# GNN kernel, last node stage: the output stores move from ACT to SP, one gated half from ACT to DVE, and one POOL add is halved

## The chip, the cores and the metric

The kernel runs on one core of a Trainium2 chip. The metric is the device time of one execution in microseconds (us). A core has five engines that run their own instruction streams and wait for one another through semaphores: TensorE (PE), VectorE (DVE), ScalarE (ACT), GpSimd (POOL) and SyncE (SP), which here only issues transfers. 16 DMA engines move the data between HBM and the on-chip memory (SBUF). PE writes its results to PSUM, which DVE and ACT can read.

## What is computed

Four graph layers follow each other. Each adds a message-passing term to the 50,000 node rows of 160 floats, and normalizes the rows:

```python
x = _layernorm(x + _L0_gnn_ref(x, ...))
x = _layernorm(x + _L1_gnn_ref(x, ...))
x = _layernorm(x + _L2_gnn_ref(x, ...))
x = _layernorm(x + _L3_gnn_ref(x, node_vec1, node_vec1_n2, node_vec1_n3, ...))
return x
```

In the last layer the part that a node computes from its own row is gated by two scalars of the node, `node_attr` and `node_crystal_attr`:

```python
def fctp_scalar_attr(xs, xv, attr, Ws, Wv):
    s = xs * attr @ Ws
    v = jnp.einsum('nuc,uo->noc', xv * attr[:, :, None], Wv)
    return (s, v)
ssa, sva = fctp_scalar_attr(xs, xv, node_attr, Ws_sc_a, Wv_sc_a)
ssc, svc = fctp_scalar_attr(xs, xv, node_crystal_attr, Ws_sc_c, Wv_sc_c)
s_s, s_v = (ssa + ssc, sva + svc)
...
agg = jax.ops.segment_sum(edge_feat, edge_dst, num_segments=n) / np.sqrt(NUM_NEIGHBORS)
...
out_s = C_S * s_s + C_X * o_s
out_v = C_S * s_v + C_X * o_v
```

So a new row is: old row + summed messages + attr0 * (x W_a) + attr1 * (x W_c), and then the layer norm over its 160 columns.

## The kernel before

Each layer has an edge stage (98 pairs of edge tiles) and a node stage. The change touches only the node stage of the last layer (`l == 3`). It works on 100 blocks of 512 nodes; a block is a tile of 128 partitions with four rows of 160 columns side by side (`BT = 4`, index `j` or `t`; row slot `j` is one node per partition). Old rows and later results of a block live in place in `xn`, a ring of eight blocks (`NRING = 8`), and the summed messages in `an`, also a ring of eight. Both are views of the SBUF tensor `arena`, so the profile names them `arena`.

Each engine has its own function of the block step `b`, and the code orders the work of different blocks within one step by hand, with lags. The steady steps are a hardware loop (`steps`, eight block steps in one loop body, 88 of the 100 blocks); the steps before and after it are written out. In the last layer:

- SP, `node_loads(b)`: waits until the store of block b-8 has landed (`stored`), loads the rows of block b into `xn` (L455, the internal table `x_after`), waits for `x_added` of block b-6, and loads the messages of block b+2 (L476, `aggregates`).
- PE, `node_products(b)`: transposes block b (L853), then multiplies block b-1 by the two weight matrices (L892, 16 matmuls). The products land in four PSUM banks, `bank[4]` to `bank[7]`, one for each row slot j; columns 0 to 159 of a bank belong to gate 0 (g = 0), columns 160 to 319 to gate 1. There is one set of banks: banks 4 and 5 may be overwritten after DVE has read them (`y_stt`), banks 6 and 7 after ACT has (`second_gated`).
- ACT, `node_copies(b)`: issues the store of block b-5 (L1020), copies the transposed block b to `nT` (L1024), multiplies the four halves of slots 2 and 3 of block b-1 by their gates and writes them to `second` (L1037, 128x160 each, named `same_all` in the profile), takes the square root for block b-3 (L1043, `std`), and normalizes slots 0, 1 and 2 of block b-4 (L1049, three instructions, `normed`).
- DVE, `node_vectors(b)`: adds the gated halves of slots 0 and 1 of block b to `xn` (`products`, four SCALAR_TENSOR_TENSOR, L1364), then in `statistics` of block b-1: the first of four bn_stats (L1380), then `inverse()` of block b-2 (L1341, waits for `std_ready`), two bn_stats, `negated_mean()` of block b-2 (L1346, writes `shift` from `mv` and `rstd`), the fourth bn_stats; then four bn_aggr (L1391).
- POOL, `add_both(b)`: normalizes slot 3 of block b-4 (L676, `last_normed`), adds the messages to all of block b (L682, 640 columns, `x_added`), and adds the two gates' results for slots 2 and 3 of block b-1 from `second` (L688 and L691, 320 columns each, `second_added`).

The square root that `inverse()` waits for in DVE's step b is the one that ACT takes in its step b+1, behind the gated halves of block b:

```python
def inverse():
    if l and within(b, late, NBLK + late):      # late is 2 in the last layer
        dve.wait_ge(std_ready, b + ((l - 1) * NBLK + 1 - late))
        nc.vector.reciprocal(rstd[:, ki, :], std[:, ki, :]).then_inc(rstd_ready, 1)
```

Of the kernel before, what the change touches and what calls it, by code (L numbers as in the profile page):

```python
# [38 lines left out]
X_EARLY = 4  # L39
XGR = 4  # L40
# [137 lines left out]
def build(nc, nodes, front, back_rows, gate_rows, pairs, first4, eattr, main, small, self_rows, mark_rows, out):  # L178
# [3 lines left out]
    with ctx:  # L182
# [185 lines left out]
        def node_count(l, b):  # L368
            return b + (l * NBLK + 1)
# [20 lines left out]
        def _(sp):  # L390
# [23 lines left out]
            for l in range(4):  # L414
# [36 lines left out]
                arows = agg.rearrange("(b p t) c -> b p (t c)", p=P, t=BT)  # L451

# [26 lines left out]
                def node_loads(b, k, turn):  # L479
                    if isinstance(b, int) and b == 0:  # L480
                        for n in range(A_LEAD[l]):
                            aggregate_load(n, n)
                    if not isinstance(b, int) or b >= X_EARLY:
                        wait(sp, stored[k], node_slot(l, k, turn - 1) * 16)
                        alone(sp, passed["sp"])
                        row_load(b, k)
                    if within(b, 0, NBLK - A_LEAD[l]):
                        aggregate_load(b + A_LEAD[l], (k + A_LEAD[l]) % NRING)

                steps(sp, 0, NBLK, NODE_STEADY if l else LOADS_STEADY, node_loads, NRING)  # L490
# [5 lines left out]
        def _(gp):  # L496
# [35 lines left out]
            for l in range(4):  # L532
# [136 lines left out]
                def add_both(b, k, turn):  # L669
# [13 lines left out]
                    if within(b, 1, NBLK + 1):  # L683
                        gp.wait_ge(second_gated, b)
                        gp.wait_ge(x_added, b + NBLK)
                        alone(gp, passed["gp"])
                        x = xn[:, place(kk)].rearrange("p (t c) -> p t c", t=BT)[:, 2:4]
                        gp.tensor_tensor(x, x, second[:, kk % XGR, 0:2], ALU.add).then_inc(first_added, 1)  # L688
                        gp.wait_ge(first_added, b)
                        alone(gp, passed["gp"])  # L690
                        gp.tensor_tensor(x, x, second[:, kk % XGR, 2:4], ALU.add).then_inc(second_added, 1)  # L691
# [223 lines left out]
        def _(act):  # L915
# [14 lines left out]
            for l in range(4):  # L930
# [76 lines left out]
                to = out if l == 3 else xtab[l + 1]  # L1007
                orows = to.rearrange("(b p t) c -> b p (t c)", p=P, t=BT)

                def node_copies(b, k, turn):  # L1010
                    if within(b, STORE_LAG[l], NBLK + STORE_LAG[l]):
                        kk, tt = back(k, turn, STORE_LAG[l], NRING)
                        done = b - STORE_LAG[l]
                        if not isinstance(b, int):
                            done = act.snap(done)
                        act.wait_ge(normed, node_count(l, b - STORE_LAG[l]))
                        if l == 3:
                            act.wait_ge(last_normed, b - (STORE_LAG[3] - 1))
                        alone(act, passed["act"])
                        act.dma_start(orows[bass.ds(done, 1)].rearrange("o p c -> (o p) c"), xn[:, place(kk)]).then_inc(stored[kk], 16)  # L1020
# [8 lines left out]
                    if l == 3 and within(b, 1, NBLK + 1):  # L1029
# [5 lines left out]
                        for g in range(2):  # L1035
                            for j in (2, 3):
                                last = nc.scalar.activation(second[:, kk % XGR, 2 * g + j - 2, :], bank[4 + j][:, g * F:(g + 1) * F],  # L1037
                                                            ACT.Copy, scale=attr[:, kk, j, g:g + 1])
# [18 lines left out]
        def _(dve):  # L1057
# [137 lines left out]
            for l in range(4):  # L1195
# [102 lines left out]
                def node_vectors(b, k, turn):  # L1298
# [50 lines left out]
                    def products():  # L1349
# [7 lines left out]
                        if l == 3:  # L1357
                            dve.wait_ge(sc_ready, base + 1)
                            for g in range(2):
                                for j in range(2):  # L1360
                                    if g == 1:
                                        dve.wait_ge(half_done, b * 2 + (j + 1))
                                    row = xn[:, place(k), j * F:(j + 1) * F]
                                    stt(out=row, in0=bank[4 + j][:, g * F:(g + 1) * F], scalar=attr[:, k, j, g:g + 1], in1=row,  # L1364
                                        op0=ALU.mult, op1=ALU.add).then_inc(half_done if g == 0 else y_stt, 1)
                            return
# [117 lines left out]
```

## Time and profile before

| | before |
|---|---|
| median of 3 runs | 3911.85 us (3908.62 to 3913.18) |
| the profiled execution | 3914.43 us, span 3912.6 us |
| busy share of the span | PE 89%, DVE 69%, POOL 64%, ACT 56% |
| last node stage, about 3482 us to the end | some 430 us, 11% of the span |
| its steady loop, 3520 to 3880 us | PE 292.85, POOL 322.35, ACT 287.19, DVE 267.56 us busy in 360 us |

The profile lists for one execution every instruction with its engine, its line and its start. "SPq" and "ACTq" are transfers that the SP and ACT queues issue; "idle before" is the time in which an engine stood still just before an instruction, and the name behind the arrow is what ended it. DVE and ACT instructions overlap their predecessor by a little, so a sum of durations is more than the time they take in a row.

### The profile page before, as it was taken

The page shows a single profiled execution, that of the slowest core. Times are in us where ns is not written, and L with a number is a line of the kernel's source. Part 1 is how long each engine was busy: PE and PEld are TensorE (multiplying, and loading weights), DVE is VectorE, ACT ScalarE, POOL GpSimd, SP SyncE. Part 2 cuts the span into 40 slices and gives each one's busy share as a digit, 9 for nine tenths or more (in the row PEclk, how much of TensorE's full clock was granted, in tenths as well). Part 3 has the DMA queues.
Part 4 walks back from the last instruction along what each step waited for, and adds up shares of the span by engine and source line. Part 5 has one row for each costly group of instructions (what it writes and reads, how often), then busy time and mean ns, then how long its engine had stood idle before and what let it go on. Part 6 is the DMA issues. An engine that isn't in the chain of part 4 may idle for free.

```text
span 3912.6 us, 103757 instructions
## 1 busy us (share of the span) xinstructions
PE 3477.1 (89%) x26652; PEld 3218.3 (82%) x26652; DVE 2710.7 (69%) x10501; ACT 2205.7 (56%) x6014; POOL 2489.7 (64%) x2969
## 2 busy tenths in 40 slices
PE   2799998666599999999979999999989999988886
PEld 2799997565499999877779999877779999987775
DVE  3577775888766666588856666588866666657776
ACT  0244443666544444477745555577756666657777
POOL 1477776888667777566667777400046666658887
PEclk9899998888799999999989999999989999999999
DMA  8622223777522222499822222388832222237775
GB/s 353 248 63 62 61 53 101 255 253 258 180 58 59 57 56 50 118 303 299 287 76 63 61 59 55 93 293 298 297 97 55 53 52 50 45 99 243 239 246 199
DMA packets 424012, 572.02 MB, mean 146 GB/s; under 512 B 218794, under 2 KB 242344, under 8 KB 419590
## 3 DMA queue, kind: packets, MB, share of 16 engines
q1 hardware_dynamic: 280742, 289.28, 25.3%
q10 hardware_dynamic: 61488, 166.57, 10.9%
q0 software_dynamic: 81680, 114.98, 10.8%
q8 instruction: 43, 0.70, 0.1%
q14 instruction: 59, 0.48, 0.0%
HBM read 356.01 MB, written 233.79 MB: 151 GB/s over the span
## 4 chain that ended last, share of the span: by engine, by line
PE 59%; ACT 11%; issue 10%; DVE 7%; DMA 5%; POOL 4%; ACTq 2%; DVEq 1%; POOLq 0%; SPq 0%
PE bank L771 17%; PE bank L804 13%; ACT arena L1049 6%; PE bank L814 5%; PE bank L761 4%; PE bank L827 3%; PE bank L824 3%; PE bank L778 3%; PE bank L819 3%; PE bank L796 3%; ACT same_all L1037 2%; POOL mark_ring L638 2%; DVE stats L1380 2%; ACTq L1020 2%; DVE arena L1373 2%
## 5 line engine op out<-in xcount | busy, mean ns | idle before, releaser
L558 POOL DMA_INDIRECT aggregates<-arena,meta x784 | 790.7, 1008 | 459.7 <-issue 252.1
L771 PE MATMUL bank<-same_all,msg 128*98 (+1 forms) x6272 | 758.6, 275 | 0.0
L545 POOL DMA_INDIRECT xg<-x_after,meta x588 | 585.8, 996 | 252.1 <-issue 247.4
L771 PEld LDWEIGHTS bank<-same_all,msg 128*98 128x98 f32 x6272 | 715.8, 167 | 0.1
L1049 ACT ACTIVATE arena<-arena,shift,rstd 128x160 f32<-128x160 f32 x1500 | 658.4, 513 | 64.1 <-DVE shift L1315 61.5
L961 ACT ACTIVATE w<-bank 1x162 f32<-1x162 f32 (+1 forms) x784 | 257.8, 329 | 741.5 <-PE bank L804 737.6
L804 PE MATMUL bank<-w,arena 98*128 98x32 f32 (+1 forms) x4704 | 628.3, 270 | 0.0
L804 PEld LDWEIGHTS bank<-w,arena 98*128 98x128 f32 x4704 | 590.1, 193 | 0.0
L1380 DVE BATCH_NORM_STATS2 stats<-arena 128x6 f32<-128x160 f32 x1600 | 454.3, 313 | 42.9 <-DVE arena L1373 8.9
L1024 ACT ACTIVATE nT<-bank 128x640 f32<-128x640 f32 x400 | 281.8, 705 | 330.3 <-PE bank L883 179.6
L1268 DVE TENSOR_TENSOR arena<-bank,yv 128x192 f32<-128x192 f32 x294 | 105.1, 358 | 477.9 <-PE bank L824 294.2
L883 PEld LDWEIGHTS bank<-sc_cols,nT 128*128 128x128 f32 x2400 | 329.3, 204 | 86.4 <-issue 86.4
L892 PE MATMUL bank<-sc_cols,nT 128*128 128x128 f32 (+4 forms) x1600 | 277.7, 327 | 77.7 <-DVE arena L1364 72.5
L892 PEld LDWEIGHTS bank<-sc_cols,nT 128*128 128x128 f32 x1600 | 240.2, 192 | 119.2 <-issue 98.0
L883 PE MATMUL bank<-sc_cols,nT 128*128 128x128 f32 (+1 forms) x2400 | 336.2, 286 | 0.0
L853 PE MATMUL bank<-ident,arena 128*128 128x128 f32 x2000 | 299.7, 283 | 32.1 <-DMA arena<-nodes 21.9
L1226 DVE COPY arena<-bank 98x512 f32<-98x512 f32 x392 | 268.7, 685 | 77.0 <-PE bank L771 64.4
L1373 DVE SCALAR_TENSOR_TENSOR arena<-bank,attr,arena 128x160 f32<-128x160 f32 x800 | 261.5, 378 | 66.3 <-PE bank L883 35.9
L761 PE MATMUL bank<-ident,xg 128*128 128x128 f32 x1176 | 208.2, 287 | 102.4 <-DMA xg<-back_rows,meta 52.1
L949 ACT ACTIVATE arena<-bank 98x512 f32<-98x512 f32 x392 | 232.0, 592 | 77.9 <-PE bank L771 77.6
L853 PEld LDWEIGHTS bank<-ident,arena 128*128 128x128 f32 x2000 | 241.9, 153 | 39.6 <-issue 38.8
L954 ACT ACTIVATE arena<-bank 128x128 f32<-128x128 f32 (+1 forms) x392 | 129.7, 331 | 235.7 <-PE bank L778 233.4
(156 smaller groups left out, 7264.2 us busy)
## 6 DMA issues: line engine op xcount, KB each, us to landing
arena<-aggregates SPq DMA_DIRECT2D x400, 324.0 KB, 4.1
x_after<-arena ACTq DMA_DIRECT2D x300, 320.0 KB, 3.9
arena<-x_after SPq DMA_DIRECT2D x300, 320.0 KB, 3.6
aggregates<-arena ACTq DMA_DIRECT2D x25, 1296.0 KB, 14.7
arena<-nodes SPq DMA_DIRECT2D x100, 320.0 KB, 3.9
out<-arena ACTq DMA_DIRECT2D x100, 320.0 KB, 3.8
same_all<-sorted_dst SPq DMA_DIRECT2D x7, 1792.0 KB, 10.9
aggregates<-arena,meta POOLq DMA_INDIRECT x784, 2.3
```

Source lines behind the costliest of these rows:

```text
L545: gp.indirect_dma_start(xg[:, k % XGR, 4 + t * F:4 + (t + 1) * F], None, xtab[l], at).then_inc(gathered[k], 16)
L558: gp.indirect_dma_start(agg, at, tot[:, kk % TRING, t, 0:AW], None, bounds_check=NP - 1, oob_is_err=False).then_inc(spread[kk], 16)
L761: last = nc.tensor.transpose(bank[0][:, c * P:(c + 1) * P], xg[:, k % XGR, 4 + c * CH:4 + (c + 1) * CH], ident[:, :])
L771: last = nc.tensor.matmul(bank[5 + t][0:MR, c * P:(c + 1) * P], msg[:, k2, t, c, :], same_all[:, bass.ds(here[t], P)], start=True, stop=True)
L804: last = nc.tensor.matmul(to, aggT[:, t, (d + 1) * P:(d + 2) * P], of, start=True, stop=True)
L853: last = nc.tensor.transpose(to[:, c * P:(c + 1) * P], xn[:, place(k), c * CH:(c + 1) * CH], ident[:, :])
L883: last = mm(A[:, o:e], turned_x[c], sc[l][:, o:e], start=fresh, stop=fresh or c == 3)
L892: return mm(two(bank[4 + j][:, 0:2 * F], F)[:, :, lo:hi], turned_x[c], W[:, :, at:at + hi - lo], **flags)
L1024: nc.scalar.activation(nT[:, k % 2, :], two_banks[k % 2][:, 0:5 * P], ACT.Copy).then_inc(nturned_out, 1)
L1049: last = nc.scalar.activation(row, row, ACT.Identity, bias=shift[:, kk, t:t + 1], scale=rstd[:, kk, t:t + 1])
L1373: last = stt(out=row, in0=ob[:, o:o + F], scalar=gate, in1=row, op0=ALU.mult, op1=ALU.add)
L1380: last = nc.vector.bn_stats(stats[:, ks % 2, j, :], xn[:, place(ks), j * F:(j + 1) * F])
```

## The change

Three pieces of work move, all in the last layer only.

1. SP issues the stores of the output. In its step b it waits for `normed` and `last_normed` of block b-7 (`OUT_LAG = 7`) and issues that store, and only then goes on to the wait, the load of block b and the message load that it had before. ACT issues no store in this layer.
2. The half g = 0 of slot 2 is no longer gated by ACT. DVE adds it to `xn` in place with a fifth SCALAR_TENSOR_TENSOR, behind its four. ACT gates the other three halves, in the order (g, j) = (0, 3), (1, 3), (1, 2), and waits before the last of them for DVE's fifth (`half_done`, which now counts three for each block).
3. POOL's first add covers slot 3 alone (160 columns), its second slots 2 and 3 as before (320 columns).

```diff
--- before.py
+++ after.py
@@ -37,6 +37,7 @@
 QUAD = 4
 NRING = 8
 X_EARLY = 4
+OUT_LAG = 7
 XGR = 4
 AW = 2 + F
 AW3 = 2 * F
@@ -449,6 +450,7 @@
 
                 xrows = xtab[l].rearrange("(b p t) c -> b p (t c)", p=P, t=BT)
                 arows = agg.rearrange("(b p t) c -> b p (t c)", p=P, t=BT)
+                out_rows = out.rearrange("(b p t) c -> b p (t c)", p=P, t=BT)
 
                 def row_load(b, k):
                     at = b if isinstance(b, int) else sp.snap(b)
@@ -480,6 +482,21 @@
                     if isinstance(b, int) and b == 0:
                         for n in range(A_LEAD[l]):
                             aggregate_load(n, n)
+                    if l == 3 and within(b, OUT_LAG, NBLK + OUT_LAG):
+                        kk, tt = back(k, turn, OUT_LAG, NRING)
+                        done = b - OUT_LAG
+                        if not isinstance(b, int):
+                            done = sp.snap(done)
+                        scaled, fourth = node_count(l, b - OUT_LAG), b - (OUT_LAG - 1)
+                        if not isinstance(b, int):
+                            scaled, fourth = sp.snap(scaled), sp.snap(fourth)
+                        sp.wait_ge(normed, scaled)
+                        alone(sp, passed["sp"])
+                        sp.wait_ge(last_normed, fourth)
+                        alone(sp, passed["sp"])
+                        sp.dma_start(out_rows[bass.ds(done, 1)].rearrange("o p c -> (o p) c"), xn[:, place(kk)]).then_inc(stored[kk], 16)
+                    if not within(b, 0, NBLK):
+                        return
                     if not isinstance(b, int) or b >= X_EARLY:
                         wait(sp, stored[k], node_slot(l, k, turn - 1) * 16)
                         alone(sp, passed["sp"])
@@ -487,7 +504,7 @@
                     if within(b, 0, NBLK - A_LEAD[l]):
                         aggregate_load(b + A_LEAD[l], (k + A_LEAD[l]) % NRING)
 
-                steps(sp, 0, NBLK, NODE_STEADY if l else LOADS_STEADY, node_loads, NRING)
+                steps(sp, 0, NBLK + (OUT_LAG if l == 3 else 0), NODE_STEADY if l else LOADS_STEADY, node_loads, NRING)
             for k in range(NRING):
                 sp.wait_ge(stored[k], 16 * 4 * node_uses[k])
 
@@ -684,11 +701,11 @@
                         gp.wait_ge(second_gated, b)
                         gp.wait_ge(x_added, b + NBLK)
                         alone(gp, passed["gp"])
-                        x = xn[:, place(kk)].rearrange("p (t c) -> p t c", t=BT)[:, 2:4]
-                        gp.tensor_tensor(x, x, second[:, kk % XGR, 0:2], ALU.add).then_inc(first_added, 1)
+                        x = xn[:, place(kk)].rearrange("p (t c) -> p t c", t=BT)
+                        gp.tensor_tensor(x[:, 3], x[:, 3], second[:, kk % XGR, 1], ALU.add).then_inc(first_added, 1)
                         gp.wait_ge(first_added, b)
                         alone(gp, passed["gp"])
-                        gp.tensor_tensor(x, x, second[:, kk % XGR, 2:4], ALU.add).then_inc(second_added, 1)
+                        gp.tensor_tensor(x[:, 2:4], x[:, 2:4], second[:, kk % XGR, 2:4], ALU.add).then_inc(second_added, 1)
 
                 def node_moves(b, k, turn):
                     if l and k % 2 == 0 and within(b, 0, NBLK):
@@ -1004,18 +1021,15 @@
                     nc.scalar.activation(waves[:, four, 1, :], trig[:, four, 0], ACT.Sin, scale=-1.0,
                                          bias=half_pi[:, :]).then_inc(sin_ready, QUAD)
 
-                to = out if l == 3 else xtab[l + 1]
-                orows = to.rearrange("(b p t) c -> b p (t c)", p=P, t=BT)
+                orows = xtab[min(l + 1, 3)].rearrange("(b p t) c -> b p (t c)", p=P, t=BT)
 
                 def node_copies(b, k, turn):
-                    if within(b, STORE_LAG[l], NBLK + STORE_LAG[l]):
+                    if l < 3 and within(b, STORE_LAG[l], NBLK + STORE_LAG[l]):
                         kk, tt = back(k, turn, STORE_LAG[l], NRING)
                         done = b - STORE_LAG[l]
                         if not isinstance(b, int):
                             done = act.snap(done)
                         act.wait_ge(normed, node_count(l, b - STORE_LAG[l]))
-                        if l == 3:
-                            act.wait_ge(last_normed, b - (STORE_LAG[3] - 1))
                         alone(act, passed["act"])
                         act.dma_start(orows[bass.ds(done, 1)].rearrange("o p c -> (o p) c"), xn[:, place(kk)]).then_inc(stored[kk], 16)
                     if within(b, 0, NBLK):
@@ -1032,10 +1046,11 @@
                         act.wait_ge(attr_copied, node_count(l, b - 1))
                         act.wait_ge(sc_ready, 2 * (b + l * NBLK))
                         alone(act, passed["act"])
-                        for g in range(2):
-                            for j in (2, 3):
-                                last = nc.scalar.activation(second[:, kk % XGR, 2 * g + j - 2, :], bank[4 + j][:, g * F:(g + 1) * F],
-                                                            ACT.Copy, scale=attr[:, kk, j, g:g + 1])
+                        for g, j in ((0, 3), (1, 3), (1, 2)):
+                            if j == 2:
+                                act.wait_ge(half_done, b * 3)
+                            last = nc.scalar.activation(second[:, kk % XGR, 2 * g + j - 2, :], bank[4 + j][:, g * F:(g + 1) * F],
+                                                        ACT.Copy, scale=attr[:, kk, j, g:g + 1])
                         last.then_inc(second_gated, 1)
                     if l and within(b, SQRT_LAG[l], NBLK + SQRT_LAG[l]):
                         kk, tt = back(k, turn, SQRT_LAG[l], NRING)
@@ -1359,10 +1374,14 @@
                             for g in range(2):
                                 for j in range(2):
                                     if g == 1:
-                                        dve.wait_ge(half_done, b * 2 + (j + 1))
+                                        dve.wait_ge(half_done, b * 3 + (j + 1))
                                     row = xn[:, place(k), j * F:(j + 1) * F]
                                     stt(out=row, in0=bank[4 + j][:, g * F:(g + 1) * F], scalar=attr[:, k, j, g:g + 1], in1=row,
                                         op0=ALU.mult, op1=ALU.add).then_inc(half_done if g == 0 else y_stt, 1)
+                            dve.wait_ge(sc_ready, base + 2)
+                            row = xn[:, place(k), 2 * F:3 * F]
+                            stt(out=row, in0=bank[6][:, 0:F], scalar=attr[:, k, 2, 0:1], in1=row,
+                                op0=ALU.mult, op1=ALU.add).then_inc(half_done, 1)
                             return
                         for d, tiles in enumerate(((3,), (0, 1, 2)) if l == 0 else ((0, 1), (2, 3))):
                             dve.wait_ge(sc_ready, base + (d + 1))
```

How the instructions stand on DVE in one step of the steady loop. Before, from the start of `products` to the first reciprocal (`arena<-bank,attr,arena` are the gated halves that are added to `xn`):

```order
L1364 SCALAR_TENSOR_TENSOR arena<-bank,attr,arena 128x160 [waits sc_ready]
L1364 SCALAR_TENSOR_TENSOR arena<-bank,attr,arena 128x160
L1362 REGISTER_ALU
L1364 SCALAR_TENSOR_TENSOR arena<-bank,attr,arena 128x160 [waits half_done]
L1362 REGISTER_ALU
L1364 SCALAR_TENSOR_TENSOR arena<-bank,attr,arena 128x160 [waits half_done]
L1401 REGISTER_ALU [waits second_added]
L1380 BN_STATS stats<-arena 128x6 [waits y_stt]
L1340 REGISTER_ALU
L1341 RECIPROCAL rstd<-std 128x4 [waits std_ready]
```

Now, from DVE's fourth to the same reciprocal:

```order
L1379 SCALAR_TENSOR_TENSOR arena<-bank,attr,arena 128x160 [waits half_done]
L1381 REGISTER_ALU
L1383 SCALAR_TENSOR_TENSOR arena<-bank,attr,arena 128x160 [waits sc_ready]
L1420 REGISTER_ALU [waits second_added]
L1399 BN_STATS stats<-arena 128x6 [waits y_stt]
L1355 REGISTER_ALU
L1356 RECIPROCAL rstd<-std 128x4 [waits std_ready]
```

The fifth (L1383) stands between the four and the reciprocal; nothing behind it has changed.

ACT in one step of the steady loop before, from the end of `normed` to the normalization (`same_all<-bank,attr` are the gated halves):

```order
L1018 REGISTER_ALU [waits normed]
L1020 ISA [waits last_normed]
L1020 DMA out<-arena 128x640
L1022 REGISTER_ALU
L1024 ACTIVATE nT<-bank 128x640 [waits sc_ready,nturned]
L1033 REGISTER_ALU [waits attr_copied,second_added]
L1037 ACTIVATE same_all<-bank,attr 128x160 [waits sc_ready]
L1037 ACTIVATE same_all<-bank,attr 128x160 x3
L1043 ACTIVATE std<-mv,eps 128x4 [waits mv_ready]
```

And now:

```order
L1036 REGISTER_ALU
L1038 ACTIVATE nT<-bank 128x640 [waits sc_ready,nturned]
L171 REGISTER_ALU
L1047 REGISTER_ALU [waits attr_copied,second_added]
L1052 ACTIVATE same_all<-bank,attr 128x160 [waits sc_ready]
L1052 ACTIVATE same_all<-bank,attr 128x160
L1051 ISA
L1052 ACTIVATE same_all<-bank,attr 128x160 [waits half_done]
L1058 ACTIVATE std<-mv,eps 128x4 [waits mv_ready]
```

The wait for `normed` and the store are gone, one gated half is gone, and the third waits for `half_done` with the square root behind it.

SP in one step of the steady loop before:

```order
L455 ISA [waits stored1]
L455 DMA arena<-x_after 128x640
L170 REGISTER_ALU
L476 ISA [waits x_added]
L476 DMA arena<-aggregates 128x648
```

And now:

```order
L495 REGISTER_ALU [waits normed]
L497 ISA [waits last_normed]
L497 DMA out<-arena 128x640
L457 ISA [waits stored1]
L457 DMA arena<-x_after 128x640
L171 REGISTER_ALU
L478 ISA [waits x_added]
L478 DMA arena<-aggregates 128x648
```

The store of block b-7 stands ahead of both loads, with its two waits, and all three go through SP's queue.

## Rows read from the trace of the kernel before

**Rows 1.** Busy time of each engine in a stretch, clock, DMA share: the steady loop.

```profile
3520.00:3880.00 360.00, 292.85 (x1860) 254.72 (x1859) 267.56 (x1237) 287.19 (x796) 322.35 (x399) 1.00 0.74 241
```

**Rows 2.** The output's stores in the loop: count, first and last start.

```profile
L1020 ACTq DMA_DIRECT2D out<-arena x88: 343/343/379, 3521.7 to 3876.3; - x88
```

**Rows 3.** Order of time, one block: start, length (us), engine, instructions, idle before.

```profile
3705.46 1.26 DVE L1364 SCALAR_TENSOR_TENSOR arena<-bank,attr,arena 128x160 f32<-128x160 f32 x4
...
3705.59 0.47 POOL L676 TENSOR_SCALAR arena<-arena,rstd,shift 128x160 f32<-128x160 f32 x1
3705.67 0.70 ACT L1024 ACTIVATE nT<-bank 128x640 f32<-128x640 f32 x1 [0.82 <-PE bank L892]
3706.03 1.43 POOL L682 TENSOR_TENSOR arena<-arena 128x640 f32<-128x640 f32 x1
3706.27 1.24 ACT L1037 ACTIVATE same_all<-bank,attr 128x160 f32<-128x160 f32 x4
...
3706.87 2.75 PE L892 MATMUL bank<-sc_cols,nT 128*128 128x256 f32 x16 [0.66 <-DVE arena L1364]
3706.88 0.33 SPq L455 DMA_DIRECT2D arena<-x_after  x1
3707.38 0.32 ACT L1043 ACTIVATE std<-mv,eps 128x4 f32<-128x4 f32 x1
...
3707.57 1.35 ACT L1049 ACTIVATE arena<-arena,shift,rstd 128x160 f32<-128x160 f32 x3
3707.74 0.18 DVE L1341 RECIPROCAL rstd<-std 128x4 f32<-128x4 f32 x1 [0.78 <-ACT std L1043]
3707.77 0.87 POOL L688 TENSOR_TENSOR arena<-arena,same_all 128x320 f32<-128x320 f32 x1 [0.31 <-ACT same_all L1037]
...
3708.27 0.39 DVE L1346 SCALAR_TENSOR_TENSOR shift<-mv,rstd 128x4 f32<-128x4 f32 x1
...
3708.82 0.86 POOL L691 TENSOR_TENSOR arena<-arena,same_all 128x320 f32<-128x320 f32 x1 [0.18 <-POOL arena L688]
3709.04 0.38 DVE L1391 BATCH_NORM_AGGREGATE mv<-stats 128x2 f32<-128x6 f32 x4
...
3709.22 0.35 ACTq L1020 DMA_DIRECT2D out<-arena  x1
3709.54 0.38 DVE L1364 SCALAR_TENSOR_TENSOR arena<-bank,attr,arena 128x160 f32<-128x160 f32 x1
...
3709.75 0.70 ACT L1024 ACTIVATE nT<-bank 128x640 f32<-128x640 f32 x1 [0.83 <-PE bank L892]
```

**Rows 4.** Who waited for whom in the steady loop: us in total, times, longest.

```profile
DVE rstd L1341 <- ACT std L1043: 66.5, 89, 1.1
PE bank L892 <- DVE arena L1364: 65.9, 88, 1.2
```

**Rows 5.** In order of time, the drain: from DVE's aggregates to ACT's root.

```profile
3901.30 0.38 DVE L1391 BATCH_NORM_AGGREGATE mv<-stats 128x2 f32<-128x6 f32 x4
...
3901.71 0.30 ACT L1043 ACTIVATE std<-mv,eps 128x4 f32<-128x4 f32 x1 [0.53 <-DVE mv L1391]
```

**Rows 6.** L1346, ns min/median/max: layers 1 and 2, then the steady loop.

```profile
L1346 DVE SCALAR_TENSOR_TENSOR shift<-mv,rstd x200: 141/145/174, 1640.8 to 2859.6; 128x4 f32<-128x4 f32 x100
...
L1346 DVE SCALAR_TENSOR_TENSOR shift<-mv,rstd x89: 331/387/394, 3520.7 to 3879.4; 128x4 f32<-128x4 f32 x89
```

**Rows 7.** A store, and the transposes behind the load that waited for it.

```profile
3701.09 0.34 ACTq L1020 DMA_DIRECT2D out<-arena  x1
...
3709.98 0.30 PE L853 MATMUL bank<-ident,arena 128*128 128x128 f32 x1 [0.36 <-DMA arena<-x_after]
```

**Rows 8.** Transfers issued in the loop: queue, count, KB each, median us to landing.

```profile
arena<-aggregates SPq DMA_DIRECT2D x88, 324.0 KB, 3.9
arena<-x_after SPq DMA_DIRECT2D x88, 320.0 KB, 3.1
out<-arena ACTq DMA_DIRECT2D x88, 320.0 KB, 3.9
```

## The prediction

> **What bounds the kernel now.** The change touches only the last node stage, so the busy shares of the whole span say little. I first read the busy times of its steady loop [rows 1] and the stores in it [rows 2]: 88 stores start from 3521.7 to 3876.3 us, so a block takes (3876.3 - 3521.7) / 87 = 4.076 us, and 360 us hold 88.3 blocks. Per block PE is busy 3.32 us, DVE 3.03, ACT 3.25, POOL 3.65. None fills 4.076, so the order within a block has to be read [rows 3].
>
> ACT first. Its rows follow each other without a gap that another engine makes: from the copy to nT (3705.67) to the gated halves 0.60, to the root (3707.38) 1.11, to the normalization (3707.57) 0.19, its three instructions 1.35 (to 3708.92), then 0.83 until the next copy at 3709.75. The sum is 4.08, the whole period. In the last 0.83 the queue waits for ACT's own `normed` and issues the store (3709.22). The row names PE, whose products end at 3706.87 + 2.75 = 3709.62; but by the code the copy of block b waits for the products of block b-2, which were through a period earlier. What stands directly ahead of the copy is the store. ACT's instruction stream sets the pace.
>
> The others wait for it. DVE's reciprocal waits for ACT's root in each block, 66.5 / 89 = 0.75 us; PE waits 0.75 us for DVE's adds [rows 4]; POOL's first add waits a little for the gated halves (0.31 idle in its row, of which some 0.17 is its own queue) [rows 3].
>
> One more thing matters. L1346 (`shift`) takes 0.145 us in layers 1 and 2, and 0.387 in this loop [rows 6]. In the order of time it runs from 3708.27 to 3708.66, and POOL's L688 ends at 3707.77 + 0.87 = 3708.64 [rows 3]. So DVE's instruction, which reads `mv` and `rstd` from SBUF, stands until POOL's add is through: 0.24 us on DVE's path in each block.
>
> The Trainium skill, "SBUF — State Buffer", section "Who interferes with whom", says that a DVE instruction with two SBUF inputs and a GpSimd instruction that reads SBUF exclude each other for a whole instruction, and that the one issued first wins. The rows here agree: 0.387 against 0.145.
>
> **The change part by part.** I count from the start of DVE's adds of a block (3705.46 in the rows) as 0.
>
> *ACT.* It loses the store with its wait (0.83 becomes about 0.1, by the distances between its other instructions) and one gated half ((1.24 - 0.40) / 3 = 0.28 us apart). Its own work is then 0.60 + 0.83 + 0.19 + 1.35 + 0.1 = 3.07 us per block. By itself this would free the whole loop.
>
> *DVE and the new wait.* The fifth add stands behind four that begin (1.26 - 0.38) / 3 = 0.295 us apart, so it begins at 1.18 and ends at 1.56. It waits for all of PE's products, which are done by then: they start 0.15 after DVE's fourth add of the block before and take 2.75 [rows 3], that is 1.41 + 2.75 = 4.16 after that block's 0, or 0.1 to 0.4 in this one. ACT's last gated half now waits for that fifth add. Behind it in ACT's stream stands the root, and for that root DVE's reciprocal waits *in the same step*. So there is a closed path:
>
> - fifth add ends: 1.56
> - ACT begins its last half: +0.03. The nearest row of a wait of ACT for DVE: the bn_aggr end at 3901.30 + 0.38 = 3901.68, the root starts at 3901.71 [rows 5]. Bounds: 0.03, and 0.15 as between DVE's fourth add and PE's products (3706.72 to 3706.87). I take 0.03, the same pair of engines.
> - the root starts 0.28 behind it and takes 0.32, the reciprocal starts 0.04 later (3707.70 to 3707.74): 2.23
> - from the reciprocal to the next block's adds: 1.80 today (3707.74 to 3709.54).
>
> With 1.80 the period would be 4.03, almost the 4.076 of today: the store's 0.83 is given back to the new wait.
>
> *POOL and `shift`.* But the 1.80 contain the 0.24 of waiting for L688. The add is now 160 columns wide. No row has that add; 640 columns take 1.43 and 320 take 0.87, which extrapolates to 0.59, and the 160-column normalization L676 takes 0.47 [rows 3]. I take 0.52, with these as bounds. ACT's last half starts at 1.59 and lasts 0.40; POOL starts 0.26 behind its end (3707.51 to 3707.77), at 2.25, and ends at 2.77 (2.72 to 2.84). `shift` is ready 0.53 after the reciprocal (3707.74 to 3708.27), at 2.76. So it meets the very end of that add or none, and waits 0 to 0.1 us. The second add starts 0.18 behind the first, at 2.95, when `shift` (0.145) is over. The 1.80 become 1.56, and the period 2.23 + 1.56 = **3.79 us**.
>
> *Is anything else slower than 3.79?* POOL: 3.65 busy less 0.35 for the halved add, plus two waits of 0.18 for its own results: 3.66. PE 3.32, DVE 3.03 + 0.3 = 3.33 plus small own waits, ACT 3.07. No, but POOL is near.
>
> *SP.* This is the cover that I cost at nothing. The store of block n now leaves when `normed` comes, as before: ACT ends its normalization at 1.59 + 0.28 + 0.19 + 1.35 = 3.41, and 0.3 for the wait (3708.92 to 3709.22) gives 3.71. Behind the store, and behind its waits, are queued the load of block n+7 and the messages, and PE waits for that load. An issue takes 0.33; with the waits I estimate 0.7 from store to load. The load lands 3.1 us after its issue, or 3.9 if it queues behind the store as the messages queue behind the load today [rows 8]: 7.5 to 8.3. PE must begin the transposes of block n+7 some 0.7 before the products of block n+6, which start 1.41 after the 0 of block n+5, two periods on: 7.58 + 1.41 - 0.7 = 8.3. It fits, with 0 to 0.8 us left. Every load also waits for the store eight blocks back: median 3.9 us to landing [rows 8], but one took 5.8 (3701.09 to the load at 3706.88), and PE then waited 0.36 at 3709.98 [rows 3, 7].
>
> The Trainium skill, "DMA: Bandwidth & Descriptors", section "Issuing engines are not separate DMA queues", holds that transfers share the same 16 engines whoever issues them, and that several issuers save only the issue time. By it the landing would not change with the queue (3.1, not 3.9); the sum is the same.
>
> *The sum.* 88 blocks x (4.076 - 3.79) = 25 us. The 12 blocks outside the loop have the same path; few of them run at full pace, and I give them 1 us. The profiled execution took 3914.4 (span 3912.6), so it would take 3888; the median of the runs is 2.6 lower, which gives **3886 us**.
>
> **The rivals.**
>
> *A, the forecast:* 3.79. Its own range: POOL's 3.66 on one side (-11 us); on the other the 0.15 for the wait (+0.12 x 88 = +10.6): 3875 to 3897. Chance 0.60.
>
> *B, the load is late but not much.* If each store landed after 5.8 us and the load after 3.1, as in the pair above, the transposes come 8.9 after the store of eight blocks back, and that must fit in three periods + 0.7 - 3.7: period 3.97, 3902 us. For it: such pairs occur. Against: they occur when SP issues two pairs of loads at once, and SP now goes in step with ACT; in the whole loop DMA has 0.26 of its time free [rows 1]. Chance 0.13.
>
> *C, no gain.* Either `shift` goes on waiting 0.24 us (POOL's add starts later than I think, because POOL comes late from its 640-column add), which gives 4.03 and 3908 us, or the waits on both sides cost 0.1 more each. Chance 0.15.
>
> *D, slower.* `shift` comes to POOL just after the second add has begun, and stands for all its 0.86. The point: POOL's first add and the 0.18 behind it must end before 2.76, so the first would have to take under 2.76 - 2.25 - 0.18 = 0.33 us; the nearest rows say 0.47 to 0.59. Price: a second add from 2.74 to 3.60, so `shift` ends at 3.62 instead of 2.90, the period is 3.79 + 0.72 = 4.51, and the time 3912 + 0.43 x 88 = 3950 us. Or the load queues (3.9) behind stores that take 5.8: 9.7, period 4.23, 3925 us. Chance 0.12 together.
>
> The skill's rule of exclusion, named above, is what makes D possible: by it the order of issue decides, and the wait is for a whole instruction.
>
> **How the numbers follow.** A measurement of this kernel can tell about 0.2% (8 us) from no change; that is 0.09 us per block, so a period under 3.99 counts as faster. A and B: faster 0.73; C: same 0.15; D: slower 0.12. The time is that of A. The range leaves out D and 0.05 below: 3877 to 3911.
>
> **What would show it.** In the loop after: stores 3.79 us apart; ACT idle before the last of three gated halves, waiting for DVE's fifth add, and no longer before nT; the reciprocal still waiting for the root, some 0.45 us (2.23 less the end of the bn_stats ahead of it, at 1.18 + 0.295 + 0.3); L1346 at 0.15 to 0.25 us instead of 0.387; PE's wait for DVE down to about 0.45. Wrong would be: L1346 at 0.39 or more, or PE or POOL waiting for loads in most blocks, or the 128x160 add far from 0.52.

## The result

| | before | after |
|---|---|---|
| median of the runs, us | 3911.85 (3908.41 to 3913.76, 5 runs) | 3886.79 (3882.35 to 3888.55, 5 runs) |
| span of the profiled execution, us | 3912.6 | 3886.7 |
| granted TensorE clock of the execution | 0.967 | 0.966 |

The ratio is 0.9936, 95% interval 0.9921 to 0.995: 25 us faster, where 26 were predicted. In another set of runs it was 0.993 (0.9916 to 0.9943).

First, the first section of the page of the changed kernel (busy time, share of the span, instructions), and its busy times in a stretch of the steady loop, in the columns of [rows 1]:

```profile
PE 3480.6 (90%) x26652; PEld 3220.3 (83%) x26652; DVE 2718.1 (70%) x10601; ACT 2187.9 (56%) x5914; POOL 2459.0 (63%) x2969
```

```profile
3520.00:3840.00 320.00, 277.61 (x1769) 242.06 (x1768) 258.69 (x1261) 258.21 (x672) 278.76 (x378) 1.00 0.76 260
```

In 100 us PE is now busy 86.8 us instead of 81.3, and POOL 87.1 instead of 89.5: the block got shorter, and POOL's share fell although it does more blocks. How long a block is can be read from any instruction that occurs once in it. For `shift`, in that stretch (minimum, median and maximum in ns, then the first and the last start):

```profile
L1361 DVE SCALAR_TENSOR_TENSOR shift<-mv,rstd x84: 143/145/148, 3523.4 to 3839.9; 128x4 f32<-128x4 f32 x84
```

That makes (3839.9 - 3523.4) / 83 = 3.813 us a block, against 4.076. Every block time below is this division, from the same kind of row. 88 x (4.076 - 3.813) = 23 us, nearly all of the gain. And `shift` takes 0.145 us instead of 0.387 [rows 6]: it never waits for POOL.

One block of the changed kernel in order of time, against [rows 3]:

```profile
3699.94 1.26 DVE L1379 SCALAR_TENSOR_TENSOR arena<-bank,attr,arena 128x160 f32<-128x160 f32 x4
...
3701.12 0.38 DVE L1383 SCALAR_TENSOR_TENSOR arena<-bank,attr,arena 128x160 f32<-128x160 f32 x1
...
3701.53 0.40 ACT L1052 ACTIVATE same_all<-bank,attr 128x160 f32<-128x160 f32 x1 [0.39 <-DVE arena L1383]
3701.82 0.29 ACT L1058 ACTIVATE std<-mv,eps 128x4 f32<-128x4 f32 x1
...
3702.14 0.18 DVE L1356 RECIPROCAL rstd<-std 128x4 f32<-128x4 f32 x1 [0.41 <-ACT std L1058]
3702.18 0.53 POOL L705 TENSOR_TENSOR arena<-arena,same_all 128x160 f32<-128x160 f32 x1 [0.33 <-ACT same_all L1052]
...
3702.67 0.15 DVE L1361 SCALAR_TENSOR_TENSOR shift<-mv,rstd 128x4 f32<-128x4 f32 x1
...
3702.88 0.86 POOL L708 TENSOR_TENSOR arena<-arena,same_all 128x320 f32<-128x320 f32 x1 [0.18 <-POOL arena L705]
3703.20 0.38 DVE L1410 BATCH_NORM_AGGREGATE mv<-stats 128x2 f32<-128x6 f32 x4
...
3703.70 1.26 DVE L1379 SCALAR_TENSOR_TENSOR arena<-bank,attr,arena 128x160 f32<-128x160 f32 x4
3703.72 0.36 SPq L497 DMA_DIRECT2D out<-arena  x1
...
3704.34 0.33 SPq L457 DMA_DIRECT2D arena<-x_after  x1
```

From 3699.94 to 3703.70 are 3.76 us. The closed path of the prediction stands in these rows: fifth add, ACT's last half 0.03 behind its end (3701.50 to 3701.53), root, reciprocal at 2.20, and 1.56 to the next adds. `shift` starts at 3702.67, 0.04 before the 160-column add ends (3702.71), and is over at 3702.82, 0.06 ahead of the start of the second add; it fits in between, narrowly. The chain that ended last (start, us, what) runs through the same places:

```profile
3704.88 0.38 DVE arena L1383
3705.58 0.29 ACT std L1058
3705.90 0.18 DVE rstd L1356
3706.08 0.44 DVE stats L1399 x2
```

The waits in the stretch, in the columns of [rows 4], and those of SP:

```profile
PE bank L909 <- DVE arena L1379: 39.1, 78, 0.8
ACT same_all L1052 <- DVE arena L1383: 35.4, 81, 0.8
DVE rstd L1356 <- ACT std L1058: 35.2, 84, 0.6
...
DVE arena L1379 <- issue: 4.9, 10, 0.5
...
PE bank L870 <- DMA arena<-x_after: 3.1, 4, 1.4
```

```profile
SPq L176 <- ACT arena L1064: 140.3, 84, 2.1
```

ACT now waits 35.4 / 81 = 0.44 us a block for the fifth add; the reciprocal waits 0.42 for the root instead of 0.75; PE waits 0.50 for DVE instead of 0.75, and only 4 times for a load. What the prediction does not have is the row "issue": 10 times in 84 blocks DVE's adds start up to 0.5 us late with no releaser. Two of those places are 3555.61 and 3586.05, eight blocks apart:

```profile
3555.61 1.26 DVE L1379 SCALAR_TENSOR_TENSOR arena<-bank,attr,arena 128x160 f32<-128x160 f32 x4 [0.50 <-issue]
3586.05 1.26 DVE L1379 SCALAR_TENSOR_TENSOR arena<-bank,attr,arena 128x160 f32<-128x160 f32 x4 [0.49 <-issue]
```

This is where the hardware loop of eight block steps turns. That block takes 4.13 us, the seven others 3.76, and the mean is 3.81. The kernel before has the same idle time (11 times, up to 0.5 us; there the profile names PE behind it), but its DVE waited 0.75 us for the root in each block anyway.

### The profile page after: what moved, and what is told of

The parts are those of the page before. It is cut to its first block, busy times and chain, and to the rows that moved or that the text cites. A ratio compares the mean times of both kernels' runs of the same rounds, so it can differ in the third digit from the quotient of the medians.

```text
span 3886.7 us, 104123 instructions
## 1 busy us (share of the span) xinstructions
PE 3480.6 (90%) x26652; PEld 3220.3 (83%) x26652; DVE 2718.1 (70%) x10601; ACT 2187.9 (56%) x5914; POOL 2459.0 (63%) x2969
## 4 chain that ended last, share of the span: by engine, by line
PE 59%; DVE 11%; issue 10%; ACT 7%; DMA 5%; POOL 4%; ACTq 1%; DVEq 1%; SPq 1%; POOLq 0%
PE bank L788 17%; PE bank L821 13%; PE bank L831 5%; ACT arena L1064 4%; PE bank L778 4%; PE bank L844 3%; PE bank L841 3%; PE bank L795 3%; PE bank L836 3%; DVE stats L1399 3%; PE bank L813 3%; POOL mark_ring L655 2%; DVE mv L1410 1%; ACT nT L1038 1%; DVE arena L1392 1%
```

## The experiments

The first four kernels ran on one chip beside the kernel before (3910.57 us there).

### One part alone

The first of two leaves only the stores on SP. Against the changed kernel, shortened (the fifth add itself goes too, and `half_done` counts two a block again):

```diff
-for g, j in ((0, 3), (1, 3), (1, 2)):
-    if j == 2:
-        act.wait_ge(half_done, b * 3)
+for g in range(2):
+    for j in (2, 3):
...
-dve.wait_ge(sc_ready, base + 2)
-stt(out=row, in0=bank[6][:, 0:F], ...)
...
-gp.tensor_tensor(x[:, 3], x[:, 3], second[:, kk % XGR, 1], ALU.add)
+gp.tensor_tensor(x[:, 2:4], x[:, 2:4], second[:, kk % XGR, 0:2], ALU.add)
```

> The change with only its first part: SP issues the output's stores; ACT gates all four halves and waits for nothing of DVE; POOL adds 320 columns twice. Theory (closed path through the fifth add and ACT's root, and POOL's narrower add frees shift): ACT's own work falls to 0.60 + 1.11 + 0.19 + 1.35 + 0.1 = 3.35 us per block, but POOL still needs 3.65 busy and two waits of 0.18, 4.01 us. So POOL becomes the bound, a period of 4.0 to 4.03, 3905 to 3908 us, nearly nothing gained; shift still waits (L1346's line at 0.3 or more). Rival 1 (the store on ACT was the whole price, so its removal is the whole gain): a period of 3.8, about 3886 us.

3887.89 us (3885.57 to 3889.47), ratio 0.9944 (0.993 to 0.9958). My theory was wrong, its rival right. POOL's rows in order of time show why:

```profile
3697.75 0.86 POOL L708 TENSOR_TENSOR arena<-arena,same_all 128x320 f32<-128x320 f32 x1 [0.18 <-POOL arena L705]
3698.56 0.21 POOL L591 COPY attr<-gate_all 128x24 f32 x1
3698.74 0.48 POOL L693 TENSOR_SCALAR arena<-arena,rstd,shift 128x160 f32<-128x160 f32 x1
3699.18 1.43 POOL L699 TENSOR_TENSOR arena<-arena 128x640 f32<-128x640 f32 x1
3700.57 0.86 POOL L705 TENSOR_TENSOR arena<-arena,same_all 128x320 f32<-128x320 f32 x1
3701.61 0.87 POOL L708 TENSOR_TENSOR arena<-arena,same_all 128x320 f32<-128x320 f32 x1 [0.18 <-POOL arena L705]
3702.47 0.47 POOL L693 TENSOR_SCALAR arena<-arena,rstd,shift 128x160 f32<-128x160 f32 x1
3702.91 1.42 POOL L699 TENSOR_TENSOR arena<-arena 128x640 f32<-128x640 f32 x1
```

POOL is back to back here (L699 ends at 3700.61, L705 starts at 3700.57), but for the 0.18 in which its second add waits for the first. From L708 to L708 are 3.86 us with the small COPY of every other block, from L693 to L693 3.73 without it: 3.80 in the mean. The measured block is 3.83; the rest is a wait of the first add at the turns of the loop, 10 times in 84 blocks. In the kernel before, the first add stood still ahead of nearly every block:

```profile
POOL arena L688 <- ACT same_all L1037: 14.0, 45, 0.3
POOL arena L688 <- POOL arena L682: 7.8, 43, 0.2
```

```profile
POOL arena L705 <- POOL arena L699: 2.3, 10, 0.2
```

The first two rows are of the kernel before, the third is of this one. I had taken 0.18 of that idle time for POOL's own, since the profile names POOL's 640-column add behind it, and so counted 4.01. Here it is gone in all blocks but those at the turns: it was a wait for ACT's gated halves, which are now done when POOL comes to them. What is POOL's own is 3.62 busy (302.52 us in 320) and the one wait of 0.18, 3.80. `shift` waits longer than before here (median 0.420 us, up to 0.692), and it costs nothing, since POOL sets the pace.

The second leaves the stores on ACT and makes only the rest of the change (`act.dma_start(orows...)` with its wait for `last_normed` stays in `node_copies`).

> The change with its second and third part: DVE's fifth add, ACT's three halves with the wait, POOL's 160 columns; but ACT issues the output's stores as before. Theory: ACT's own work is 0.60 + 0.83 + 0.19 + 1.35 + 0.83 = 3.80 us per block, and the closed path is 3.76 as in the changed kernel; a period of 3.80 to 3.85, 3888 to 3893 us. So nearly the whole gain comes without SP. Rival 1 (the store's removal is the gain): a period of 4.0 or more, 3905 us or more. Rival 2 (without the stores on SP the waits add up, ACT waits for DVE and then issues): 3.95, 3900 us.

3884.86 us (3884.2 to 3890.36), ratio 0.9939 (0.9925 to 0.9952); `shift` takes 0.145 us. Its block is (3836.9 - 3517.8) / 83 = 3.84 us. That is 20 us of the gain in 88 blocks. The times alone can't tell either part from the whole change. A finer measure is the stretch from the first to the last `shift` of the stage in each profile, which leaves out the stages ahead (they end up to 8 us apart from one execution to another): 396.3 us before, 370.8 in the changed kernel (370.3 in the profile of its other set), 375.6 and 374.5 with one part alone. So either part alone brings some 21 us, and both together 25:

| kernel | stores | halves on ACT | POOL's first add | block | first to last `shift` | time, us |
|---|---|---|---|---|---|---|
| before | ACT | 4 | 320 | 4.08 | 3506.0 to 3902.3 | 3910.57 |
| stores only | SP | 4 | 320 | 3.83 | 3498.0 to 3873.6 | 3887.89 |
| half only | ACT | 3 | 160 | 3.84 | 3499.9 to 3874.4 | 3884.86 |
| changed | SP | 3 | 160 | 3.81 | 3505.6 to 3876.4 | 3886.79 (set of the result) |

Before, ACT's stream of 4.08 stood alone. Less the store it is under 3.8, less a half it is 3.80; and right below lie POOL with its two wide adds at 3.80 and, once the half has moved, the closed path at 3.76 with its turn, 3.81. There are three bounds within 0.05 us. (Why the kernel with the half only takes 3.84 and not 3.81 was not separated; its PE waits 25 times in the stretch for a load.)

### The width of POOL's first add

The changed kernel with a first add of 320 columns, which adds a stale half to slot 2, and with one of 16 columns, which leaves the rest of slot 3's half out:

```diff
-gp.tensor_tensor(x[:, 3], x[:, 3], second[:, kk % XGR, 1], ALU.add)
+gp.tensor_tensor(x[:, 2:4], x[:, 2:4], second[:, kk % XGR, 0:2], ALU.add)
```

> The changed kernel, but POOL's first add covers 320 columns again; its second slot then adds a stale half to slot 2, so the output is not the reference's. Theory: shift waits for the end of POOL's first add again, 0.35 to 0.39 us instead of 0.145, which makes the closed path 3.76 + 0.22 = 3.98, and POOL's own work is 4.01; a period of 4.0 to 4.05, 3905 to 3910 us. Rival (the narrow add matters for nothing, since POOL was not the bound in the kernel before): 3887 us, and shift stays at 0.145.

```diff
-gp.tensor_tensor(x[:, 3], x[:, 3], second[:, kk % XGR, 1], ALU.add)
+gp.tensor_tensor(x[:, 3, 0:16], x[:, 3, 0:16], second[:, kk % XGR, 1, 0:16], ALU.add)
```

> The changed kernel, but POOL's first add covers only 16 of the 160 columns of slot 3 (the rest of that half is left out). Less work than in the changed kernel. Theory: POOL's first add takes 0.22 to 0.25 us, so its second begins 0.28 us earlier, at 2.6 us behind the start of DVE's adds, ahead of shift at 2.73; shift then stands until the second add ends, 2.61 + 0.87 = 3.48, and takes 0.75 instead of 0.145; a period of 3.76 + 0.6 = 4.36, about 3940 us, slower than the kernel before. Rival (POOL and DVE do not exclude each other; only work and order count): POOL has 0.3 us less to do, the period stays 3.76, 3887 us or a little less, and shift stays at 0.145.

| first add, columns | its time | `shift`, median | block | time, us | ratio |
|---|---|---|---|---|---|
| 320 | 0.86 | 0.385 | 4.00, with turns 4.05 | 3905.31 | 0.9989 (0.998 to 0.9999) |
| 160 | 0.53 | 0.145 | 3.76, with turns 3.81 | 3886.79 | 0.9936 (0.9921 to 0.995) |
| 16 | 0.22 | 0.783 | 4.40, with turns 4.44 | 3943.99 | 1.0087 (1.0071 to 1.0102) |

With a tenth of the work in its first add the kernel is slower than before. In order of time, the kernel with 16 columns:

```profile
3707.69 0.22 POOL L705 TENSOR_TENSOR arena<-arena,same_all 128x16 f32<-128x16 f32 x1 [1.03 <-ACT same_all L1052]
...
3708.09 0.87 POOL L708 TENSOR_TENSOR arena<-arena,same_all 128x320 f32<-128x320 f32 x1 [0.18 <-POOL arena L705]
3708.19 0.79 DVE L1361 SCALAR_TENSOR_TENSOR shift<-mv,rstd 128x4 f32<-128x4 f32 x1
```

POOL's second add has started 0.10 us ahead of `shift`; `shift` ends at 3708.98, 0.02 behind the end of that add (3708.96). This is what rival D describes. The excess of `shift` over 0.145 is 0.64 here and 0.24 with 320 columns, and the block without turns grows by as much: 4.40 - 3.76 = 0.64, 4.00 - 3.76 = 0.24. So the 0.24 us are on the closed path, and the halved add is what takes them off it. The rule of exclusion in the Trainium skill, "SBUF — State Buffer", section "Who interferes with whom", agrees with all three rows.

### The order on ACT, and the lag of the stores

These ran on another chip, on which the kernel before takes 4698 us (why, was not looked into), so only ratios and block times are compared. The first takes the closed path apart: ACT takes its root ahead of the gated half that waits for DVE. Shortened, with the root taken out of its old place:

```diff
 for g, j in ((0, 3), (1, 3), (1, 2)):
     if j == 2:
+        square_root()        # std for block b-3
         act.wait_ge(half_done, b * 3)
```

> The changed kernel, but ACT takes the square root ahead of its last gated half, so the root no longer stands behind the wait for DVE's fifth add. Theory (the path fifth add, ACT's last half, root, reciprocal is the bound): the reciprocal comes right behind the first bn_stats, 1.7 us behind the start of DVE's adds instead of 2.2; shift is ready at 2.25 and now meets POOL's first add (2.22 to 2.75) and waits to its end, so it takes about 0.5 us instead of 0.145; a steady block of 1.73 + 1.56 + 0.37 = 3.66 instead of 3.76, about 3877 us. Rival (POOL, PE or the transfers are the bound at 3.76, not that path): 3886 us, and the reciprocal no longer waits for the root but something else idles DVE.

Ratio 0.9891 (0.9856 to 0.9926), mean block (4588.1 - 4311.6) / 79 = 3.50:

```profile
L1367 DVE SCALAR_TENSOR_TENSOR shift<-mv,rstd x80: 144/278/355, 4311.6 to 4588.1; 128x4 f32<-128x4 f32 x80
```

The reciprocal waited for the root 7 times in 80 blocks instead of in every block. The block is shorter than the 3.66 that I expected, for `shift` waits less: 0.278 us in the median and not 0.5. What sets the pace is POOL, whose own work is less than I had counted, as the first experiment had begun to show: in the stretch it waits for ACT twice, and otherwise for nothing but its own results.

The next kernel stores one step earlier (`OUT_LAG = 6`), so that SP waits longer for the normalization with the next load queued behind:

> The changed kernel with OUT_LAG = 6: SP waits for and stores block b-6 ahead of the load of block b, one block later in ACT's order. Theory (the stores on SP are covered by less than one block of slack): the load of block n+6 leaves 3.71 + 0.7 us behind the start of DVE's adds of block n+3 and lands 3 us later, at 7.4, where PE needs it one period + 0.7 behind that start; so the period would have to become about 6.7 us, and the kernel 100 us slower at least, up to 4170 us. Rival (SP runs far ahead, the lag has more than a block to spare): 3887 us as with a lag of 7.

Ratio 1.042 (1.0382 to 1.0457), mean block 6.10, where I expected 6.7. SP's waits and PE's, in a stretch of its loop:

```profile
SPq L176 <- ACT arena L1064: 209.4, 53, 7.2
```

```profile
PE bank L870 <- DMA arena<-x_after: 98.8, 27, 4.0
```

The cover that I costed at nothing is thus less than one block step: without it each second block waits up to 4 us for its rows. With a lag of 7 no run shows a cost; with a lag of 6 the block takes 6.10 us against 3.81.

The third has the root first and `shift` behind the fourth bn_stats. On DVE, beside the first one's edit on ACT:

```diff
 if j == 0:
     inverse()
-if j == 2:
+if j == (3 if l == 3 else 2):
     negated_mean()           # shift
```

> The kernel with the root ahead of ACT's last half, and in the last layer DVE computes shift behind the fourth bn_stats instead of ahead of it. Theory: shift is then issued at about 2.6 us, meets only the last 0.2 us of POOL's first add, and the fourth bn_stats is done while it would have waited; it still comes before POOL's second add (2.93). DVE's own order then gives 3.3 to 3.4 us, and POOL with 3.48 or PE with 3.4 becomes the bound: a steady block of 3.5 to 3.55, about 3864 to 3868 us. Rival 1 (shift now meets POOL's second add and stands 0.86 us): 4.1 or more, 3910 us or more. Rival 2 (the order of shift does not matter, only the root did): as the kernel with the root first alone.

Ratio 0.9871 (0.9843 to 0.9898), mean block (4568.6 - 4313.1) / 74 = 3.45. The expected 3.5 to 3.55 had POOL at 3.48. The ratios of the two kernels with the root first can't be told apart. The expectations below take 3.52 and 3.47 for their blocks, the rows give 3.50 and 3.45.

### The same kernels beside the changed one

On a chip where the kernel before takes 3908.84 us, the changed kernel again, the two that beat it, and the better of the two with the stores on ACT again:

> The changed kernel itself, as the yardstick for the three beside it. Its steady block is 3.76 us (4.13 at each turn of the loop, mean 3.81). On a chip like the first: 3882 to 3889 us against 3909 to 3914 before, ratio 0.993 to 0.995.

> The changed kernel with ScalarE's root issued ahead of its last gated half. By the block already seen (mean 3.52 against 3.81), 84 to 88 blocks save about 0.29 us each, 24 to 26 us: about 3861 us beside a changed kernel at 3887. If what VectorE wins is lost again ahead of the stage's end, or in the stages around it, the time stays at 3880 or above although the block is shorter.

> As the one before, and in the last node stage `shift` is issued behind the fourth bn_stats. By its block already seen (mean 3.47): 3.47 against 3.52 makes 4 us more, about 3857 us. If the 0.05 us a block is chance, it reads as the one before, 3861.

> The order of the one before, but the output's stores issued by ScalarE again (DVE's fifth add and the 160-column add stay). If ScalarE's stream with its stores is a bound of its own right under the changed kernel's path, it now decides: its work of 0.60 + 1.11 + 1.35 + 0.83 us less one gated half of 0.28 makes 3.8 us with the waits in it, against 3.47 without the stores, so the time stays near 3884 us, 25 us behind the one before. If the stores on ScalarE cost nothing here either, it reads as the one before, 3857 us.

| kernel | time, us | ratio | block | 88 blocks' saving on 3883.3 |
|---|---|---|---|---|
| changed | 3883.3 | 0.993 (0.9916 to 0.9943) | 3.81 | |
| root first | 3860.57 | 0.9868 (0.9853 to 0.9883) | 3.558 | 3861 |
| root first, shift late | 3852.65 | 0.9852 (0.9839 to 0.9866) | 3.471 | 3853 |
| the same, stores on ACT | 3879.7 | 0.993 (0.9917 to 0.9944) | 3.778 | 3880 |

All four came within 5 us of what was expected. Between root first and root first with `shift` late the block is 0.09 us shorter, but the intervals of the ratios overlap, so that `shift`'s own part in the 8 us is likely and not certain.

The `shift` rows from which the blocks are worked out, first of the one with the stores on SP, then of the one with the stores on ACT:

```profile
L1367 DVE SCALAR_TENSOR_TENSOR shift<-mv,rstd x94: 144/508/764, 3517.1 to 3839.9; 128x4 f32<-128x4 f32 x94
```

```profile
L1353 DVE SCALAR_TENSOR_TENSOR shift<-mv,rstd x87: 282/288/293, 3515.1 to 3840.0; 128x4 f32<-128x4 f32 x87
```

Here the store is worth 27 us, and with the changed kernel's order it was worth 3 to 4 (3.84 against 3.81 a block, 374.5 against 370.8 in the stage). ACT in order of time, with the stores on it:

```profile
3701.80 0.70 ACT L1024 ACTIVATE nT<-bank 128x640 f32<-128x640 f32 x1 [0.83 <-PE bank L892]
3702.40 0.67 ACT L1046 ACTIVATE same_all<-bank,attr 128x160 f32<-128x160 f32 x2
3702.95 0.30 ACT L1034 ACTIVATE std<-mv,eps 128x4 f32<-128x4 f32 x1
3703.14 0.40 ACT L1046 ACTIVATE same_all<-bank,attr 128x160 f32<-128x160 f32 x1
3703.42 1.34 ACT L1056 ACTIVATE arena<-arena,shift,rstd 128x160 f32<-128x160 f32 x3
3705.06 0.34 ACTq L1020 DMA_DIRECT2D out<-arena  x1
3705.59 0.70 ACT L1024 ACTIVATE nT<-bank 128x640 f32<-128x640 f32 x1 [0.83 <-PE bank L892]
```

The terms are those of [rows 3] with one half less: 0.60 + 0.55 + 0.19 + 0.28 + 1.34 + 0.83 = 3.79, the period. This is the second bound, shown by itself.

With the stores on SP, POOL is the bound; it is back to back again:

```profile
3700.16 0.87 POOL L708 TENSOR_TENSOR arena<-arena,same_all 128x320 f32<-128x320 f32 x1 [0.18 <-POOL arena L705]
...
3703.54 0.87 POOL L708 TENSOR_TENSOR arena<-arena,same_all 128x320 f32<-128x320 f32 x1 [0.18 <-POOL arena L705]
...
3707.07 0.87 POOL L708 TENSOR_TENSOR arena<-arena,same_all 128x320 f32<-128x320 f32 x1 [0.18 <-POOL arena L705]
```

3.38 without the COPY and 3.53 with it, 3.46 in the mean; the block takes 3.47. `shift` waits 0.36 us for POOL in the median there, off the path.

Not tried: a last half on ACT that does not wait for the fifth add. Both read PSUM bank 6 (`bank[6]`), ACT columns 160 to 319 and DVE columns 0 to 159, and nothing but that wait orders them.

## Why the prediction was right

**ACT's stream, with the store in it, sets the pace.** Right. The store moved alone gives 3887.89 us, and put back under the shortest order it costs 27 us; but a gated half taken out of the same stream saves as much. The prediction's sum of ACT's stream carried to 3.79 with three halves and stores.

**The closed path.** Right in each term. Fifth add to last half: predicted 0.03, measured 0.03. Reciprocal: 2.23 predicted, 2.20 measured. From there to the next adds: 1.56 and 1.56. Period: 3.79 predicted, 3.76 measured. With the root ahead of the half the path is gone and the block falls to 3.56.

**POOL and `shift`.** Right. The 160-column add: 0.52 predicted, 0.53 measured. `shift` meets no add. The two other widths show both sides of it: 0.24 and 0.64 us a block. Rival D was to begin with a first add under 0.33 us; at 0.22 us it came, with 4.40 us a block where the prediction had 4.51. Where it begins between 0.22 and 0.53 was not measured.

**SP's cover.** It held: store at 3.78 in the block (predicted 3.71), load 0.62 behind (0.7). The load does not queue behind the store: of the two values for its landing, 3.1 and 3.9, the longer did not come, and the median is 2.9 us. PE waited 3.1 us for loads in 84 blocks. Rival B did not come, and one step less of lag does what it describes, at a far higher price.

**What was mis-sized.** First, a term is missing from the sum, the turn of the loop: 0.37 us per eight blocks, 88 / 8 x 0.37 = 4 us. Before, it was hidden, because DVE waited in each block anyway. The period, 0.03 shorter than predicted, gave back 3 us; that the time came out within 1 us of the forecast is luck, of two small errors of opposite sign. Second, the prediction's 3.66 for POOL is 3.46. It changed nothing here, but by the same way of counting I took POOL with both adds wide for 4.01, where it is 3.80, and so expected that the stores alone would bring 3 to 7 us. That sum counted two waits of 0.18 as POOL's own, and the one ahead of the first add was a wait for ACT. Third, "the store's 0.83 is given back to the new wait" is right for the changed kernel and misleads on the parts: each removes the same bound, and either brings some 21 of the 25 us.

## What to carry to other kernels

An idle time is an engine's own only if it stays when nothing else holds the engine up: here one of two waits of 0.18 us, both put down to POOL itself, was a wait for ACT. So an engine's own minimum is only sure in a run in which it is back to back, read from start to start. When a change has several parts, price each against the next bound: here three bounds lay within 0.05 us a block, so parts that each save 21 us of the stage alone saved 25 together, and the step to 3852.65 us needed the closed path opened as well. A sum over a hardware loop also needs its turn. And before a POOL instruction is made shorter, look at which DVE instruction with SBUF inputs will then meet the next one.

## What the runs showed of the hardware

A DVE instruction on 128x4 elements with two inputs in SBUF took 0.145, 0.385 or 0.783 us, by POOL's add in flight alone, and ended 0.02 us behind that add where it was held up. Making that add a tenth as long made the kernel 57 us slower than the 160-column version (3943.99 against 3886.79). The turn of the hardware loop cost 0.37 us on DVE where it was on the path. When PE had to wait for loads (the lag of 6), its granted clock was 0.78 in the mean over a stretch of the loop, so for a part of it the engine ran at the lower of its two levels (1.2 and 2.4 GHz), and 16 products took 5.03 us (granted clock 0.52 over them) where they take 2.75 at 1.00:

```profile
4400.00:4700.00 300.00, 208.94 (x1029) 189.17 (x1030) 153.82 (x738) 150.63 (x392) 164.44 (x222) 0.78 0.49 165
```

```profile
4500.56 5.03 PE L909 MATMUL bank<-sc_cols,nT 128*128 128x256 f32 x16
```

So a part of the 6.10 us a block in that kernel is the slower clock, and not the late rows alone; how much was not separated.
